# Mixing with row-pair halves: four quarter-size projection matmuls, v in full 128-row tiles, one sum over 112 partitions, and statistics through four buffers

## The reference, cut to what matters

```python
# layer 0
qkv = depthwise3x3(conv1x1(_gn(x), qkv_w), dw_w)
q, k, v = split(qkv)            # _to_blocks: 8 heads, 96 = 6 channels x 4 x 4 positions, 128*128 tokens
attn = softmax(normalise(q) @ normalise(k).T * temperature)   # 96 x 96 for each head
x = x + conv1x1(_from_blocks(attn @ v), proj_w)
# layer 1: h[t] = x[t] + conv1d(h[t-1], w, 5 taps) + b, down, up, right, left
x = x + four_scans(_gn(x))
```

## Time and profile before

| what | value |
|---|---|
| time, median of 3 runs | 10444.34 us (10396.53 to 10444.9) |
| the profiled execution's own time | 10459.08 us |
| its span | 10457.5 us |
| TensorE busy | 9371.0 us, 90% of the span |
| VectorE busy | 8061.7 us, 77% |
| ScalarE busy | 6283.6 us, 60% |
| mean granted TensorE clock | 0.953 |

### The profile page before, as it was taken

One profiled execution on the slowest core, in us unless ns is written; L12 is line 12 of the kernel. 1 busy time (PEld: TensorE's weight loads), 2 busy tenths in 40 slices (PEclk: granted clock), 3 DMA queues, 4 the chain that ended last, 5 costly groups with the idle time before them and its releaser, 6 DMA issues. The chain is left out here.

```text
span 10457.5 us, 212639 instructions
## 1 busy us (share of the span) xinstructions
PE 9371.0 (90%) x72232; PEld 9011.2 (86%) x72232; DVE 8061.7 (77%) x16201; ACT 6283.6 (60%) x11047; POOL 2983.2 (29%) x4333
## 2 busy tenths in 40 slices
PE   2999999999999998999979999999999999999100
PEld 2999999999999997776779999999999999999100
DVE  7888888777777776887877777777799997777333
ACT  2777777777777774333456667999833336666100
POOL 0000000000000000000046666666666666666100
PEclk9999999999999999999989999999999999999655
DMA  8888887667666767999978896777766667777899
GB/s 246 169 169 168 171 169 142 127 127 135 134 133 133 135 134 162 250 240 231 258 161 196 202 199 182 214 218 211 211 208 221 208 199 190 196 202 201 341 431 415
DMA packets 783419, 2101.26 MB, mean 201 GB/s; under 512 B 58480, under 2 KB 633232, under 8 KB 698336
## 3 DMA queue, kind: packets, MB, share of 16 engines
q1 hardware_dynamic: 654928, 1744.17, 67.3%
q0 software_dynamic: 22016, 151.01, 6.0%
q10 hardware_dynamic: 106368, 204.76, 5.5%
HBM read 1344.51 MB, written 754.97 MB: 201 GB/s over the span
## 5 line engine op out<-in xcount | busy, mean ns | idle before, releaser
L1450 ACT CAST hi<-rough 112x256 fp32r<-112x256 f32 x4096 | 1666.5, 407 | 1409.0 <-DVE rough L1364 1358.2
L1284 PE MATMUL scan_ps<-hi,scan_high 112*112 112x256 f32 x12264 | 2123.7, 281 | 31.1 <-ACT hi L1450 31.1
L1364 DVE SCALAR_TENSOR_TENSOR rough<-scan_ps,scan_bias,lines 112x256 f32<-112x256 f32 x4086 | 2136.6, 523 | 18.7 <-issue 14.4
L1295 PE MATMUL scan_ps_low<-lo,scan_high 112*112 112x256 f32 x12264 | 2130.2, 282 | 1.0 <-POOL lo L1396 0.7
L1290 PE MATMUL scan_ps_low<-hi,scan_low 112*112 112x256 f32 x12264 | 2122.6, 281 | 0.0
L440 PE MATMUL conv_ps<-tap_low,x_high 128*128 128x432 f32 (+2 forms) x6144 | 1905.5, 310 | 0.0
L440 PE MATMUL conv_ps<-tap_high,x_high 128*128 128x432 f32 (+2 forms) x6144 | 1882.3, 306 | 25.8 <-DVE vt L647 14.1
L440 PE MATMUL conv_ps<-tap_high,x_low 128*128 128x432 f32 (+2 forms) x6144 | 1904.0, 310 | 0.0
L1284 PEld LDWEIGHTS scan_ps<-hi,scan_high 112*112 112x112 f32 x12264 | 1690.9, 175 | 32.3 <-ACT hi L1450 31.8
L1295 PEld LDWEIGHTS scan_ps_low<-lo,scan_high 112*112 112x112 f32 x12264 | 1684.5, 175 | 5.7 <-POOL lo L1396 2.7
L1290 PEld LDWEIGHTS scan_ps_low<-hi,scan_low 112*112 112x112 f32 x12264 | 1686.1, 176 | 0.0
(11 more groups left out here) (140 smaller groups left out, 12303.4 us busy)
## 6 DMA issues: line engine op xcount, KB each, us to landing
raw<-x SPq DMA_DIRECT2D x764, 256.0 KB, 4.7
d_rows<-lines SPq DMA_DIRECT2D x32, 3584.0 KB, 30.2
u_cols<-lines SPq DMA_DIRECT2D x64, 1792.0 KB, 13.0
r_cols<-lines SPq DMA_DIRECT2D x32, 3584.0 KB, 24.3
lines<-u_cols SPq DMA_DIRECT2D x31, 3584.0 KB, 16.5
lines<-r_cols SPq DMA_DIRECT2D x30, 3584.0 KB, 16.4
lines<-d_rows SPq DMA_DIRECT2D x30, 3360.0 KB, 15.6
v_blocks<-xs ACTq DMA_DIRECT2D x128, 768.0 KB, 4.4
```

What stands on the lines that cost most here:

```text
L1284: last = nc.tensor.matmul(ps[:, b, 0:LP], high[:, shift], hi[:, b, (k - 1) % 2, shift:shift + LP], start=shift == 0, stop=shift == 2)
L1295: last = nc.tensor.matmul(ps_low[:, b, 0:LP], high[:, shift], lo[:, b, shift:shift + LP], start=False, stop=shift == 2)
L1364: nc.vector.scalar_tensor_tensor(rough[:, b, k % 2], ps[:, b, 0:LP], bias, line(way, s, k % T, b, kept), ALU.add, ALU.add).then_inc(rough_ ...
L1450: nc.scalar.copy(hi[:, b, k % 2, 1:LP + 1], rough[:, b, k % 2]).then_inc(hi_ready[b], 1)
```

## The change

In `attention`, the chunks of the statistics are 1 MB, in four slots instead of two. Main rows and edges have semaphores of their own, and ScalarE waits for the edges only before the first edge cast. The border values are filled per slot, and at the change of batch SP loads the main rows of a slot as soon as it is free.

In the mixing, `v_blocks` keeps for each of 128 partitions the 6 tiles side by side, so that `v_in` is [128, 6 tiles] instead of [96, 8 heads]. A tile of 128 rows touches two heads, so `attT` holds, for each tile, 192 columns, with zeros where a row doesn't belong to a head; three products per bank of `a_ps` accumulate in overlapping column ranges. The weights are put in place by matmuls with a permutation, `order`, in place of the transposes. The two halves of `res`, `o_ps` and `scan_t` now hold alternate pairs of image rows, and the two banks of a pair hold columns of one parity, so that one VectorE sum covers 112 partitions x 1024 elements. For this the projection of a `turned` tile is two matmuls, one for each half of 48 input partitions, and for odd `m` the output halves are swapped. `projd` is the projection twice, one copy below the other, padded to 64 columns. The projection is one step later than before, and the transposes of a group's last step are in the next group's first step. `bn_stats` are taken once for two pairs, four at a time. `x1_scan` and the last sum follow the new order of rows; the last sum is eight adds of half the size instead of four.

Not shown below: `soft`, the tile in which the softmax is made, has zeros on both sides (GpSimd clears them), `res` is cleared instead of `scan_t` and before its first loads, `order` is a new input of 96x96, and the loops over the statistics' slots run to four. Where "..." stands in place of removed lines, the functions of the kernel before are those printed above.

```diff
+NV = HEADS * HD // 128
...
+def x1_groups(x1_scan, b):
+    return x1_scan[b].rearrange("c (g q f t w) -> c g q f t w", g=G, q=2, f=2, t=NP)
+def x1_row(t):
+    return NP * (t % N // 2) + 2 * (t // N) + t % 2
...
-    v_blocks = dram("v_blocks", (B, G, HEADS * HD, NB * TOK))
-    x1_scan = dram("x1_scan", (B, C, G, 2, T, W2))
+    v_blocks = dram("v_blocks", (B, G, 128, NV, NB * TOK))
+    x1_scan = dram("x1_scan", (B, C, G * RUN))
...
-    CH, FM = 4096, 512
+    CH, FM = 2048, 512
+    SLOTS = 4
...
                     for b in range(B):
-                        sp.wait_ge(top_filled[b], 1)
-                        if b:
-                            load(b, 0, 0, top=True)
-                            load(b, 1, 1)
-                        else:
-                            load_edge(b, 0, 0)
-                            load_edge(b, 1, 1)
+                        for s in range(2):
+                            if b:
+                                sp.wait_ge(low_ready[b - 1], NT - 1 + s)
+                                load_main(b, s, s, top=s == 0)
+                            sp.wait_ge(top_filled[b][s], 1)
+                            load_edge(b, s, s)
...
-                        act.wait_ge(raw_in[b][s], 8 * LOADS * (n - s) + 16 * LOADS)
+                        act.wait_ge(main_in[b][s], 8 * MAIN * (n - s) + 16 * MAIN)
+                    def edges_arrive(b, n, s):
+                        act.wait_ge(edge_in[b][s], 8 * EDGES * (n - s) + 16 * EDGES)
...
                             casts(3)
                             if not (first and i == 0):
                                 square(b, n - 1, i - 1, first and i == 1)
+                            if to_b < B:
+                                edges_arrive(to_b, to_n, s)
                             casts(4)
...
+                                if b + 1 < B:
+                                    v.wait_ge(low_ready[b], NT - 1)
+                                    fill_top(b + 1, 0)
                             if last and i == NB - 2 and b + 1 < B:
                                 v.wait_ge(low_ready[b], NT)
-                                fill_top(b + 1)
-                    fill_top(0)
+                                fill_top(b + 1, 1)
...
-        v_in = sb("v_in", [HD, 2, HEADS, NB, TOK])
+        soft = sb("soft", [HD, HEADS, 3 * HD])
+        v_in = sb("v_in", [128, 2, NV, NB, TOK])
...
+        projd = sb("projd", [PP, ODD])
+        order_sb = sb("order_sb", [HD, HD])
+        scan_t = sb("scan_t", [PP, 2, 2, NP, W2])
...
         def load_res(queue, b, g, s, half):
-            queue.dma_start(res[ODD * half:ODD * half + C, s],
-                            x[b, :, bass.ds(T * g + NP * half, NP)]).then_inc(res_landed[half][s], 16)
-        def store(queue, b, g, s, q):
+            rows = x[b].rearrange("c (g i f l) w -> c g i f (l w)", g=G, i=NB, f=2)
+            queue.dma_start(res[ODD * half:ODD * half + C, s].rearrange("p (i l) w -> p i (l w)", i=NB),
+                            rows[:, bass.ds(g, 1), :, half].rearrange("c g i lw -> c (g i) lw")).then_inc(res_landed[half][s], 16)
+        def store(queue, b, g, s, half):
             queue.wait_ge(summed, N * G * b + N * g + N)
-            queue.dma_start(x1_scan[b, :, bass.ds(g, 1), q].rearrange("c g t w -> c (g t) w"),
-                            scan_t[ODD * q:ODD * q + C, s]).then_inc(scan_out[q][s], 16)
+            queue.dma_start(x1_groups(x1_scan, b)[:, bass.ds(g, 1), :, half].rearrange("c g q t w -> c (g q) (t w)"),
+                            scan_t[ODD * half:ODD * half + C, s].rearrange("p q t w -> p q (t w)")).then_inc(scan_out[half][s], 16)
...
-                    sp.dma_start(v_in[:, s].rearrange("p h i n -> p h (i n)"),
-                                 v_blocks[b, bass.ds(g, 1)].rearrange("g (h p) n -> p (g h) n", p=HD)).then_inc(v_landed[s], 16)
+                    sp.dma_start(v_in[:, s].rearrange("p k i n -> p (k i n)"),
+                                 v_blocks[b, bass.ds(g, 1)].rearrange("g p k n -> (g p) (k n)")).then_inc(v_landed[s], 16)
...
                     pe.wait_ge(probs, b + 1)
-                    for h in range(HEADS):
-                        last = nc.tensor.transpose(w_ps[:, h // 4, (h % 4) * HD:(h % 4 + 1) * HD], diag[:, h], eye[0:HD, 0:HD])
+                    for tile in range(NV):
+                        for side in range(2):
+                            first = HD + (tile % 3) * (128 - HD) - HD * side
+                            at = 2 * HD * (tile % 2) + HD * side
+                            last = nc.tensor.matmul(o_ps[:, tile // 2, at:at + HD], soft[:, tile // 3 * 4 + tile % 3 + side, first:first + 128],
+                                                    order_sb[:], start=True, stop=True)
                     last.then_inc(transposed, 1)
                 pe.wait_ge(att_ready, B)
...
-                def project(j, s, ms, first):
-                    for m in ms:
-                        if not (first and m < NBANK):
-                            pe.wait_ge(summed, N * j + m // 2 - 1)
-                        nc.tensor.matmul(o_ps[:, m % NBANK], projd[:], flat(turned[:, s, m]),
-                                         start=True, stop=True).then_inc(o_done, 1)
...
+                def project(s, pair):
+                    for m in (2 * pair, 2 * pair + 1):
+                        for half in range(2):
+                            to = half if m % 2 == 0 else 1 - half
+                            wide = C if to else ODD
+                            last = nc.tensor.matmul(o_ps[ODD * to:ODD * to + wide, m % NBANK],
+                                                    projd[ODD * half:ODD * half + C, 0:wide],
+                                                    flat(turned[ODD * half:ODD * half + C, s, m]), start=True, stop=True)
+                    last.then_inc(o_done, 1)
...
+                def products(b, j, s, i, first=False):
+                    n = NB * j + i
+                    if i == 0:
+                        pe.wait_ge(v_landed[s], 8 * (j - s) + 16)
+                    if not first:
+                        pe.wait_ge(taken, n)
+                    for half in range(2):
+                        for k in (0, 2, 1):
+                            tile = 3 * half + k
+                            last = nc.tensor.matmul(a_ps[:, half, k * HD:(k + 2) * HD], v_in[:, s, tile, i, :],
+                                                    attT[:, b, tile], start=k == 0, stop=k == 1)
+                    last.then_inc(att_done, 1)
+                def start_of(b):
                     for i in range(NB):
...
+                        products(b, 0, 0, i, first=i == 0)
                         if i:
...
+                            turn(i - 1, (i - 1) % 2, first=i == 1)
+                    for i in range(NB):
+                        products(b, 1, 1, i)
+                        if i > 2:
+                            pe.wait_ge(summed, i - 2)
+                        turn(NB + i - 1, (i - 1) % 2)
+                        if i == 1:
+                            pe.wait_ge(proj_in, 32)
+                        if i:
+                            project(0, i - 1)
+                def group(b, j, s):
+                    for i in range(NB):
+                        products(b, j, s, i)
+                        pe.wait_ge(summed, N * j + i - 6)
+                        turn(NB * j + i - 1, (i - 1) % 2)
+                        project(1 - s if i else s, i - 1 if i else N - 1)
                 for b in range(B):
...
+                    if b:
+                        group(b, b * G, 0)
+                        group(b, b * G + 1, 1)
+                    else:
+                        start_of(b)
                     with pe.Fori(1, G // 2) as i:
                         group(b, b * G + 2 * i, 0)
                         group(b, b * G + 2 * i + 1, 1)
+                pe.wait_ge(summed, N * GROUPS - 6)
+                turn(NB * GROUPS - 1, (NB - 1) % 2)
+                project(0, N - 1)
                 pe.wait_ge(turn_moved, NB * GROUPS)
-                project(GROUPS - 1, 1, range(NM), False)
+                for pair in range(N):
+                    pe.wait_ge(summed, N * (GROUPS - 1) + pair - 1)
+                    project(1, pair)
...
-                def sums(b, g, s, dy, last=False):
+                    nc.vector.tensor_copy(attT[:, b].rearrange("p (f k) d -> p f (k d)", f=3),
+                                          o_ps[:, 0:3, 0:4 * HD]).then_inc(att_ready, 1)
+                def sums(b, g, s, pair):
                     j = G * b + g
...
+                    bank, low, q = 2 * (pair % 2), pair // 2, pair % 2
+                    v.wait_ge(o_done, N * j + pair + 1)
+                    nc.vector.tensor_tensor(
+                        scan_t[:, s, q, low:NP:2].rearrange("p i (j two) -> p i j two", two=2),
+                        o_ps[0:PP, bank:bank + 2].rearrange("p two (i j) -> p i j two", j=TOK),
```

(32 more changed lines are left out.)

163 lines of the change are left out of this document (67 added, 96 removed).

## The result

The changed kernel takes 10300.4 us (median of 4 runs, 10293.1 to 10309.6), the kernel before 10444.6 (median of 4, 10396.5 to 10447.8). The ratio is 0.9874, 95% interval 0.9849 to 0.9899: 1.3% faster, where the prediction said slower. The profiled execution of before (10459) lies in the upper part of that spread, slower than 62 of the 72; that of after (10302.1, span 10300.5) lies in the middle of a narrow one. So the differences between the two traces, 157 us in all, are a little larger than those between the medians.

The account below looks back on a forecast made before the run. The prediction took TensorE to bound the kernel, and argued about the mixing. Mixing +120, statistics -14, edges -4, change of batch -12, last sum +1 gave +91 us, so 10550, with the median put at 10540; range 10280 to 10780.

Parts of the forecast that it names:

- the price of the projection: Mixing step: eight small passes in five slots, since only passes on different quarters overlap; 2.15 us, +0.43 us a step.
- Products: Mixing step: 12 passes of 192 columns instead of 16 of 96, 1.93 us, +0.17 us a step.
- Switches: Mixing step: TensorE going from whole array to quarters and back, 0.27 us a step, bounds nothing and 0.54.
- start of the mixing: Placing the weights by matmuls, about +8 us, and the first projection one step later, +3.1: +11.1 us.
- Rival A: Mixing: all four quarters at once, projection 0.86 us, then transfers bind at 4.2 us a step; 10280, chance 0.22.
- Stalls: Mixing: of 104 us of stalls 5 us stay, upper bound 40, as 21.5 us landings nearly fit 20.9 us groups.
- worth nothing itself: Mixing: the 1.57 us a step freed on VectorE, an engine that does not bind, was given no gain of its own.
- clean steps, 250: Mixing: 250 steps of 1.93 + 0.87 + 2.15 + 0.27 = 5.22 us, where a clean step had taken 4.35.
- statistics: Head: four buffers of half the size keep the load queue full, -14 us, bounds 0 and -25 (VectorE's floor).
- edges, start and change of batch: Main casts run while edges land at the start, -4 us; loads issued earlier at the change of batch, -12 us.
- scans and last sum: After the mixing: scans unchanged; last sum as eight smaller adds, 9.8 instead of 9.2 us a chunk, +0.6 once.
- the tail: End of the mixing: six projections at 2.15, one transpose, a switch and the last sum, 15.9 us.

Follow-up runs that it names:

- the 72: the occasions on which the kernel before was run again in the experiments, unchanged: between 10373 and 10507 us, medians of 10419 to 10428 for each set.
- e2: changed kernel with the halves of odd row pairs not swapped, so the four small projection matmuls use two quarters of TensorE's array: 10459 us.
- e3: changed kernel, but ScalarE takes the products of a group's first step before copying the turned rows of the group before: 10243 us.
- e15: e3 with products as eight matmuls of 96 rows by 96 columns, v still loaded as 128-row tiles in 12 KB runs: 10284 us.
- e7: changed kernel with the sum of a pair split into four instructions of about 512 columns on half the partitions: 10381 us.
- e6: changed kernel with v loaded as before the change, onto 96 partitions in 2 KB runs, products keeping their tiles and durations: 10305 us.
- e8: changed kernel with the statistics back in chunks of 4096 through two buffers: 10319 us.
- e9: e3 with v back as eight heads of 96 rows, in products and load: 10370 us.
- e4: changed kernel with v kept in DRAM by tile before partition, read in 2 KB runs on 128 partitions: 10305 us.
- e14: e3 with v loaded onto 96 partitions in 2 KB runs, products keeping their tiles and durations: 10340 us.

## Why the prediction was wrong, by its steps

**The step that failed is the price of the projection**, "the second pass of a quarter goes with the first of the next: five slots instead of eight, 2.15 us". It rested on passes starting in the order of the program. The records show all four first passes within 0.02 us and all four second passes 0.47 us later; e2 shows that only passes of one quarter queue. The projection's eight passes need two slots, about 0.93 us (1.02 to the next products, with the switch) for the 2.15 forecast, 1.2 us less in each of 250 steps. The Trainium skill, "TensorE: Matmul & The Clock Gate", Part 3 on packing small matmuls, says that matmuls on different tiles overlap and start and end strictly in program order. For the first passes the trace agrees: they start 0.006 to 0.008 us apart, with 64, 48, 48 and 64 columns of weights as in the code. I had carried the rule over to the two passes of an fp32 matmul, and there it doesn't hold: all first passes come before any second, and the second passes don't keep the order of the matmuls either, since one with 48 columns starts first, at 4516.333, and the two with 64 at .341 and .360. The prediction named this sign itself, passes that "overlap more than their order allows".

**The other terms of the step held.** Products: 1.93 us for 12 passes forecast, 12 x 0.162 = 1.95 measured. Sum: 1.22 forecast, 1.23. Switches: 0.27 forecast; measured 0.09 on the way in (0.20 from the last transpose to the first `o_ps` pass, 0.11 between transposes), and on the way back about 0.09 and 0.10 more before the second pass of the products, since its weights aren't loaded ahead: 0.29. Of the drain that the Trainium skill, "TensorEngine Tiling (Array Packing)", Key Properties, describes, the trace thus shows about half of my upper bound. The Trainium skill, "TensorEngine Tiling (Array Packing)", Gotcha 1, says that different row tiles cannot access one PSUM bank at the same time; this trace shows no such wait: the first two passes come from different row halves, write partitions 0 to 63 and 64 to 111 of one bank, and start 0.006 us apart.

**A wait that I had missed.** TensorE's turn of a group's last step moved behind the next group's first products, and ScalarE's copy did not. I priced the move at the start of the mixing only. It costs 0.92 us at each of some 62 borders; without it the kernel is 57 us faster (e3).

**Rival A had the right time, 10280, for a reason that was half wrong.** Four quarters at once, yes; that transfers then bind at 4.2 us a step, no: ScalarE's order made the 4.27, and with it mended transfers carried 4.06 at 288 GB/s, and in the second half of e15 3.85 at 307. That 4.2 and 4.27 lie so close is luck. Of the mechanism I wrote that "nothing in the data orders" the outputs, and gave the order of the queue more weight than that, without a row.

**Stalls.** That TensorE's would nearly vanish was right, but I relied on 20.9 us a group. The group became 17.1 us, and they vanished all the same, though VectorE's waits for `res` did not (91.8 us for 85.8). That VectorE has room is shown to matter: the relief "worth nothing itself" is worth 81 us at this step (e7). That v lands in 12.3 us (21.6 before) is not shown to: with its old form it lands in 13.7 and nothing is lost (e6). I had read 21.5 us as what full queues give; it is a median over stretches with and without stalls.

**The sum, term by term**, profiled execution 10302 against 10550:

| term | forecast | measured |
|---|---|---|
| clean steps, 250 | 5.22 | 4.04: -295 us |
| border steps of ScalarE | none | +57 |
| stalls of TensorE | +5 | 0 |
| statistics | -14 (0 to -25) | -27 |
| edges, start and change of batch | -4, -12 | -4, -12 |
| start of the mixing | +11 | +15 |
| last sum ending to the scans' start | 0 | -8 |
| scans and last sum | +1 | +14 |

These differences, -295 + 57 - 5 - 13 + 4 - 8 + 13 and -1 in the tail, make the 248 us. (The tail was forecast at 15.9 us, but the terms named for it add up to 15.3; it measured 14.8.) The statistics end 2 us beyond their range: with four buffers VectorE is busy 95% of the time, so they came down to the floor that had given -25, where I took half of the way; and the first chunk, half as large, is in 3.1 us sooner (29.7 instead of 32.9 us), which I hadn't counted. e8 gives 26.7 for this edit. The edges and the change of batch are read from the trace alone; no run undoes them. The +14 of the last row is no effect of the change that I can name: over the profiled executions of the seventeen kernels the scans, which are the same in all but for the place of their rows, take 4396 to 4407 us from their first matmul to the last, and what follows varies by 16.

What stays open: why e9's groups fall to 256 GB/s on the mean, below what the same form of load reached in e6 (276), and why e15 runs half of the mixing with a wait in every second group and the other half with none. For e15 it is no ceiling of the rate, since its second half goes beyond it; for e9 that isn't shown.

## What to carry to other kernels

Price small matmuls by quarters of the array: passes on different quarters cost one slot together, passes on one quarter queue, so count the passes of the fullest quarter and add about 0.3 us for going there and back. When an engine's work is moved past a loop border, move its partner's too, and look at the border step by itself. A share of DMA of 1.00 is no bound by itself; ask what is late, and who has the slack to absorb it. Before a mean over a stage is called a limit, cut the stage into groups: a clean stretch in the same trace refutes the limit.

## What the runs showed of the hardware

The duration of a 2 KB packet of v depended on where it went and on what else was under way. From the packet records of 4100 to 5050 us, mean ns of one packet:

```
              v, 2 KB   v, 12 KB   other packets on the same queue
before        174       -          16 KB: 958
changed       -         742        4 KB: 238, 8 KB: 462
e4 (128 part.) 133      -          4 KB: 243, 8 KB: 443
e6 (96 part.)  154      -          4 KB: 222, 8 KB: 365
e9, e14 (96)   162      -          4 KB: 284, 276; 8 KB: 407, 372
```

768 packets of 174 ns are 8.4 us of the 16 engines a group, 128 of 742 ns 5.9. Of the 2.4 us between them, 6.4 - 5.9 = 0.5 goes with the run length (e4), some 1.0 with 96 partitions in place of 128 (e6), and the rest, it seems, with what shares the queues; no run separates that. A load of 7.4 us a group (e6) cost 5 us in a group of 17.1 us, and one of 7.8 (e14) cost 97 us in one of 16.2.
